# RNN, LSTM, shared MLP, experts and a low-rank adapter on one core: the first x tile by two transfers, the x tiles turned one to a step, and the fill work of an LSTM step dealt out anew

## The reference, cut to what matters

```python
x = x + rnn(x, h0=cond)        # h = tanh(h @ Wh + x_t @ Wx + b), 256 steps
x = x + lstm(x, h0=cond, c0=0) # gates i, f, o, g of 256 each, 256 steps
x = x + moe(x, cond)           # shared MLP 256 -> 1024 -> 256 on every token,
                               # and 2 of 4 experts of the same size, chosen per batch
x = x + adapter(x, cond)       # low rank 8, matrices made from LayerNorm(cond)
```

## Time and profile before

| what | value |
| --- | --- |
| median of 3 runs | 1104.92 us (1102.71 to 1107.42) |
| the profiled execution | 1103.3 us, of it 1101.5 us from first to last instruction |
| granted TensorE clock, mean | 0.987 of full speed |
| TensorE busy | 1064.8 us (97%) |
| VectorE, ScalarE, GpSimd busy | 75%, 59%, 26% |

### The profile page before, as it was taken

The page is one execution under the profiler, slowest core; times in us unless marked ns, Lnnn a source line. Parts: engine busy times, 40 slices in busy tenths (PEclk is TensorE's granted clock), DMA queues, the critical chain, the costliest instruction groups (busy, mean ns, idle before and its releaser), DMA issues. The chain is left out here.

```text
span 1101.5 us, 56333 instructions
## 1 busy us (share of the span) xinstructions
PE 1064.8 (97%) x22306; PEld 968.1 (88%) x22306; DVE 826.0 (75%) x3573; ACT 646.7 (59%) x2500; POOL 284.4 (26%) x862
## 2 busy tenths in 40 slices
PE   4899999999999999999999998899999999999998
PEld 3889899899999999999999997788888888888887
DVE  6577778878878878877887887876666666676797
ACT  4467767767777777777776765433333333343486
POOL 3223333333333333333333330560000000000041
PEclk9789999999999999999999999999999999999999
DMA  8401211211211200000000011100000000000022
GB/s 269 101 24 55 66 28 53 66 29 52 66 45 35 66 27 10 18 24 14 14 19 4 5 30 14 13 9 2 2 2 2 1 2 2 2 4 1 4 91 83
DMA packets 55434, 37.28 MB, mean 34 GB/s; under 512 B 25816, under 2 KB 54026, under 8 KB 55180
## 3 DMA queue, kind: packets, MB, share of 16 engines
q1 hardware_dynamic: 54316, 33.26, 10.8%
q10 hardware_dynamic: 864, 0.43, 0.2%
HBM read 28.68 MB, written 4.98 MB: 31 GB/s over the span
## 5 line engine op out<-in xcount | busy, mean ns | idle before, releaser
L670 ACT ACTIVATE gel<-bank,seq 128x256 f32<-128x256 f32 x256 | 121.2, 474 | 214.9 <-PE bank L1306 212.1
L1304 PE MATMUL bank<-XHL,WE 128*128 128x256 f16 x768 | 209.4, 273 | 2.6 <-DVE XHL L896 1.1
L1304 PE MATMUL bank<-GH,WE 128*128 128x256 f16 x768 | 209.3, 273 | 2.5 <-DVE GH L923 2.0
L1306 PE MATMUL bank<-XHL,WE 128*128 128x256 f16 x768 | 209.5, 273 | 0.0
L1305 PE MATMUL bank<-GH,WE 128*128 128x256 f16 x768 | 209.4, 273 | 0.0
L1306 PE MATMUL bank<-GH,WE 128*128 128x256 f16 x768 | 209.4, 273 | 0.0
L1305 PE MATMUL bank<-XHL,WE 128*128 128x256 f16 x768 | 209.4, 273 | 0.0
L464 POOL TENSOR_TENSOR RH<-rf,RH 128x32 f16<-128x32 f32 x256 | 73.3, 286 | 420.5 <-ACT RH L608 420.5
L1304 PE MATMUL bank<-seq 128*128 128x64 f16 (+2 forms) x1216 | 154.0, 202 | 1.8 <-DVE oz L956 1.1
L1306 PE MATMUL bank<-seq 128*128 128x64 f16 (+2 forms) x1216 | 154.5, 202 | 0.3 <-issue 0.3
L930 DVE CAST GH<-gel 128x256 f16<-128x256 f32 x256 | 78.1, 305 | 101.8 <-ACT gel L670 101.0
(11 more groups left out here) (221 smaller groups left out, 3353.9 us busy)
## 6 DMA issues: line engine op xcount, KB each, us to landing
stage<-in_L_cond_ew SPq DMA_DIRECT2D x64, 128.0 KB, 2.4
stage<-in_L_cond_W SPq DMA_DIRECT2D x32, 256.0 KB, 3.7
WE<-in_x SPq DMA_DIRECT2D x8, 512.0 KB, 10.0
out<-WE SPq DMA_DIRECT2D x16, 256.0 KB, 2.1
stage<-in_L_cond_sw SPq DMA_DIRECT2D x2, 1024.0 KB, 7.0
scratch<-rows SPq DMA_DIRECT2D x96, 8.0 KB, 1.9
stage<-in_L_cond_Wx SPq DMA_DIRECT2D x1, 1024.0 KB, 7.0
stage<-in_L_cond_Wh SPq DMA_DIRECT2D x1, 1024.0 KB, 9.4
```

Source lines behind the costliest of these rows:

```text
L670: nc.scalar.activation(gel[:, m % 2, :], banks[m % len(banks)][:, 0:256], ACT.Gelu_apprx_tanh, scale=scale, bias=bias).then_inc(s["a_g"], 1)
L1304: MM(out_, w(HI), x(HI), start=start, stop=False, skip_group_check=True)
L1306: return MM(out_, w(HI), x(LO), start=False, stop=stop, skip_group_check=True)
```

## The change

Seven edits:
1. `load_first` issues one transfer of 128 KB on each of the two queues in place of eight of 16 KB.
2. GpSimd's low halves of every second turn (k odd) move from RNN step 4k + 4 to 4k + 5.
3. In VectorE's start, the low halves of the first x tile and the copy of `lnT` move ahead of the RNN's bias rows.
4. Tiles 0 to 3 are turned beside RNN steps 3, 4, 6 and 7, tiles 4 to 7 after LSTM steps 1 to 4 of block 0, tiles 8 to 15 after steps 7 to 14 as before. Tiles 0 and 1 are copied out beside the RNN's start, 2 and 3 in step 0, 4 to 7 in steps 2 to 5.
5. `x_hi` and `x_lo` of block 0 move from steps 4, 6 and 5, 7 to steps 5, 6 and 6, 7.
6. `HALVES` and `HALVES_LOW` move half tiles out of steps 7 and 15, into 8 and 9 or into 9 and 13; `X_TILES` moves one gate tile from step 5 to step 7 of every eight.
7. `EXPERT` moves two weight pieces a block from steps 11 and 13 to 9 and 12 (blocks 9 and later); `block_sum` moves from steps 0 and 3 to 3 and 12.

```diff
-        def load_first(engine, batches):
-            for b in batches:
-                engine.dma_start(xin_first[U * (b % G):U * (b % G) + U, b // G, :], a["x"][b, 0:U, :]
+        def load_first(engine, halves):
+            for h in halves:
+                engine.dma_start(xin_first[:, h, :], a["x"][h * G:(h + 1) * G, 0:U, :]
                                  ).then_inc(s["ld_xf"], 16)
...
-                load_first(sp, range(G))
+                load_first(sp, (0,))
...
-                if n >= H and n % H == 0:
+                if n % G == H or (n > G and n % G == 1):
                     split_x1(n // H - 1, LO)
...
-                load_first(act, range(G, B))
+                load_first(act, (1,))
...
@@ ScalarE, the eight RNN steps at the start
+                if n == 5:
+                    x_out(0)
...
@@ ScalarE and VectorE, block_steps
-                    if it < NB - 1 and u in X_HI:
-                        x_hi(it + 1, X_HI.index(u))
+                    x_at = X_HI_FIRST if first else X_HI
+                    if it < NB - 1 and u in x_at:
+                        x_hi(it + 1, x_at.index(u))
...
@@ VectorE, the start
-            bias_parts(4 * D, 5 * D, S_RNN)
-            dve.sem_inc(s["v_const"], 1)
+            dve.wait_ge(s["v_xr"], 1)
+            V.tensor_tensor(XR[:, LO, 1], X[:, 1, :, 0:U].rearrange("p b t -> p t b"),
+                            XR[:, HI, 1], ALU.subtract).then_inc(s["v_xr"], 1)
             dve.wait_ge(s["pe_cond"], 2)
             V.tensor_copy(lnT[:].rearrange("p c b -> p (c b)"), cond_bank[:, C * B:2 * C * B]
                           ).then_inc(s["v_cond"], 1)
-            dve.wait_ge(s["v_xr"], 1)
-            V.tensor_tensor(XR[:, LO, 1], X[:, 1, :, 0:U].rearrange("p b t -> p t b"),
-                            XR[:, HI, 1], ALU.subtract).then_inc(s["v_xr"], 1)
+            bias_parts(4 * D, 5 * D, S_RNN)
+            dve.sem_inc(s["v_const"], 1)
             weight_lo(0, rnn_piece())
...
             for piece in range(N_LSTM):
                 weight_lo(N_RNN + piece, lstm_piece(piece))
+                if piece == 9:
+                    x_out(1)
...
@@ TensorE
-            pe.wait_ge(s["ld_xf"], 16 * B)
+            pe.wait_ge(s["ld_xf"], 16 * 2)
...
             for n in range(LAG):
                 rnn_step(n)
+                for k in X_TURN_FIRST[n]:
+                    transpose_x(k)
...
-            for k in X_OUT[0]:
-                transpose_x(k)
...
-                    if first and u + 1 < U:
-                        for k in X_OUT[u + 1]:
-                            transpose_x(k)
+                    for k in X_TURN[u] if first else ():
+                        transpose_x(k)
...
-HALVES = [0, 3, 2, 1, 3, 2, 2, 3, 0, 3, 2, 1, 3, 2, 2, 3]
-HALVES_LOW = [0, 3, 2, 1, 3, 2, 2, 3, 1, 3, 3, 1, 2, 1, 2, 3]
+HALVES = [0, 3, 2, 1, 3, 2, 2, 2, 1, 4, 2, 1, 3, 2, 2, 2]
+HALVES_LOW = [0, 3, 2, 1, 3, 2, 2, 2, 1, 4, 3, 1, 2, 2, 2, 2]
...
+X_HI_FIRST, X_LO_FIRST = (5, 6), (6, 7)
+X_TURN_FIRST = [(), (), (), (0,), (1,), (), (2,), (3,)]
+X_TURN = [(), (4,), (5,), (6,), (7,), (), (), (8,), (9,), (10,), (11,), (12,), (13,), (14,), (15,), ()]
-X_OUT = [(2 * u, 2 * u + 1) if u < 4 else (u,) if u >= 8 else () for u in range(U)]
+X_OUT = [(2, 3), (), (4,), (5,), (6,), (7,), (), ()] + [(k,) for k in range(8, 16)]
...
-           [], [("ig", 0), ("o", 0), ("o", 1)], [("f", 0), ("f", 1), ("ig", 1)], [("ig", 2), ("ig", 3)]]
-EXPERT, EXPERT_LOW = (1, 11, 13, 15), (1, 9, 12, 14, 15)
-SUMS, SUMS_LAST, ADD_Y = (0, 3), (0, 1), (1, 2)
+           [], [("o", 0), ("o", 1)], [("f", 0), ("f", 1), ("ig", 0)], [("ig", 1), ("ig", 2), ("ig", 3)]]
+EXPERT, EXPERT_LOW = (1, 9, 12, 15), (1, 9, 12, 14, 15)
+SUMS, SUMS_LAST, ADD_Y = (3, 12), (0, 1), (1, 2)
```

More of the change, by code:

```diff
@@ L1070, in block_steps @@
                         extras[u]()
-                    if it < NB - 1 and u in X_LO:
-                        x_lo(it + 1, X_LO.index(u))
+                    x_at = X_LO_FIRST if first else X_LO
+                    if it < NB - 1 and u in x_at:
+                        x_lo(it + 1, x_at.index(u))
                     for k in X_OUT[u] if first else ():
```

## The result

The changed kernel takes 1097.61 us (median of 5 runs, 1096.15 to 1098.6) against 1104.92 before, a ratio of 0.993 with a 95% interval of 0.9909 to 0.9952. Timed once more beside the experiments it took 1097.97 against 1104.37: 0.9952 (0.9935 to 0.997). So it is 6 to 7 us faster by the medians, and the time is inside the predicted range. (The ratios are estimated from all executions and are not the quotients of these medians; their intervals reach from 3 to 10 us.) The working behind the 1095 holds less well than the number. One execution of the kernel `a_sw` further down took 1866.07 us and is not counted in its ratio; why it was so slow isn't known.

The account below looks back on a forecast made before the run. Each LSTM step was taken as ended by TensorE's own list or the step's chain (floor 2.31 us). From 1103.3 us, -3.5 - 4.3 + 0.2 - 0.8 + 0.2 = -8.2 gave 1095.1 us, range 1091.5 to 1099.5.

Parts of the forecast that it names:

- start: Up to the first LSTM step: 3.1 us from earlier transfers plus 0.4 from VectorE's order, 29.31 to 25.8 us.
- these have the same company on the queues as before, so they come about 3.1 us earlier: At the start: the adapter's first weights still land 5.2 us after issue, so about 3.1 us earlier; bounds 1.5 and 3.3.
- the start gives less: Rival at the start: gain only 1.5 us, start and weights' landing slip by 1.6, total 1096.7 us; chance 0.12.
- VectorE's new order: At the start: the `lnT` copy starts at 12.7, not 13.17, bringing the first RNN product 0.4 us earlier; bounds 0 and 0.5.
- Turning the tiles: Tiles turned beside RNN steps: block 0's steps 0 to 3 need 10.3 us, with no TensorE wait for an x copy.
- the prediction's first rival: Half clock in block 0's steps 2 and 3: step 4 starts about 3 us later, total 1096.7 us; chance 0.14.
- The wait for the MLP's weights: Block 0, before step 4's gates: ScalarE waits from about 36 us for weights landing near 37.9; step 5 starts at 39.8.
- the term of step 13: Blocks 9 to 14: two VectorE operations of 0.42 us just ahead of `ig` lengthen step 13 by about 0.10 us.
- GpSimd's move: Low halves moved beside TensorE-bound steps 2 and 10 cost nothing there; bound +0.15 us in each, 4 us over 14 blocks.
- holds up `ig`: Step 1 of blocks 1 to 14: `block_sum` delays `ig`; moving it and GpSimd's low halves out of step 0 gives -0.20 us.
- The rival by which the gate tiles come too late: GpSimd's low halves come too late in step 2 or 10: 31 turns lose 0.4 us each, total 1107; chance 0.05.
- The end: Last block: a half tile moved into step 9 and a wait at the end that doesn't shrink, +0.2 us.

Follow-up runs that it names:

- a_sw: Changed kernel with SP's fourteen small tables moved from ahead of the shared MLP's weight loads to behind them; ratio 0.9902 to the kernel before.
- after: The changed kernel with all seven edits, first measurement and first trace; 1097.61 us against 1104.92 before, ratio 0.993.
- a_again: The changed kernel timed and traced again with no edit; 1097.97 us against 1104.37 before, ratio 0.9952.
- b_blocks: Kernel before with only the moved half tiles, gate tiles, GpSimd low halves, expert pieces and block sums; ratio 0.999.
- b_pool: Kernel before with only GpSimd's low halves of every second turn one RNN step later, one line; ratio 0.9967.
- b_sums: Kernel before with only VectorE's two block sums moved from steps 0 and 3 to 3 and 12; ratio 0.9975.
- b_halves: Kernel before with only the new tables of half tiles, gate tiles and expert pieces; ratio 1.0008.
- b_start: Kernel before with only the two large first x transfers and VectorE's new order at the start; ratio 0.9998.
- b_turn: Kernel before with only the new turning, copying and splitting of block 0's x tiles; ratio 0.9981.
- a_all: Changed kernel with adapter weights ahead of ScalarE's small tables, MLP weights ahead of SP's, and tiles 4 to 7 copied a step earlier; 1095.52 us, ratio 0.9914.
- a_aw1: Changed kernel with the adapter's first weights ahead of the small tables on ScalarE's queue; ratio 0.9938 to the kernel before.

## Why the number was right and what in it was wrong

The table gives each term. For what the change leaves, I take the mean of `after` and `a_again`; for the kernel before, the mean of the traces that have that part unchanged.

| term | predicted | measured | from |
| --- | --- | --- | --- |
| start | -3.5 | -1.2 | 28.78 against 29.97 (before, b_blocks, b_pool, b_sums, b_halves) |
| block 0, steps 0-3 | -5.6 | -5.7 | 10.65 against 16.33 (before, b_start, b_sums, b_halves) |
| block 0, steps 4-15 | +1.5 | +2.5 | 36.59 against 34.08 (before, b_start, b_sums) |
| blocks 1-14 | -0.8 | -3.6 | 559.44 against 563.04 (before, b_start, b_turn) |
| block 15 and after | +0.2 | +1.0 | 460.15 against 459.13 (before, b_start, b_turn) |

The measured terms add up to -7.0 us; the medians say -7.3 and -6.4. That the total fits is partly luck: the start gave 2.3 us less than forecast and blocks 1 to 14 gave 2.8 us more, from unrelated steps of the working. The measured -1.2 of the start is uncertain too, since among the five traces with the old start the first LSTM step lies between 28.89 and 30.93 us.

- **The start failed.** The step "these have the same company on the queues as before, so they come about 3.1 us earlier" was wrong. The issues moved by 2.4 and 2.9 us, since one large transfer took 1.22 and 0.80 us to issue and not 0.47. The landing moved by 0.36: 7.3 us after the issue in place of 5.2. The adapter's weights are now issued 0.74 us ahead of SP's first 1 MB transfer (3.51 and 4.25), where it was 1.2. `b_start` shows that the start alone gives nothing that its timing can tell. The term stood outside its own bound of 1.5, and the rival "the start gives less" is what happened. That the nearer 1 MB transfer delays them is argued from these rows; no run moves it alone. The working also missed that VectorE waits for these weights only by the shared count `ld_first`. VectorE's new order was right, and worth a little more than its bound of 0.5: from L879 to the `lnT` copy it takes 1.40 us instead of 1.96.
- **Turning the tiles was right**, in size too: steps 0 to 3 of block 0 at 2.30, 2.46, 2.51 and 2.92 us against 2.3, 2.7, 2.4 and 2.9, and no wait for a copy. `b_turn` shows it by itself. But these are the steps of the first trace, the only one of seven kernels built on the change that has the full clock there (`b_turn` has it too). In the other six step 2 runs partly at half clock and takes 3.4 to 3.7 us. That is the prediction's first rival in a milder form: steps 0 to 3 are 0.9 us longer in `a_again`, not 3, and the wait for the weights is shorter.
- **The wait for the MLP's weights came, and its length by luck** (1.73 us, forecast near 1.9). The forecast had ScalarE there from about 36 us and the data at 37.9; it came at 38.8 and the data at 40.45, 2.8 and 2.6 us late. SP's issue moved by 1.6 us and the landing by 0.5, since the transfer took 6.2 us in place of 5.1. What the wait costs is 0.0 to 0.4 us by the traces of `a_sw` and `a_again`. Missed was the second wait: `x_hi` needs tile 7, whose copy stands in VectorE's step 5. I had costed the crowding of these steps at 0.4 us without asking which tile `x_hi` waits for.
- **Blocks 1 to 14 were mis-sized** by 2.8 us. Step by step the sum for blocks 9 to 14 was -0.04 and came out at -0.30. Nearly all of the difference is the term of step 13: predicted +0.10, measured -0.14. I costed `block_sum` in step 12 as two more operations ahead of `ig`; `b_sums` shows that they cost nothing (2.49), and the runs of single pieces show that step 13 gains only when a gate tile and an expert piece have left it and a block sum stands in step 12. Blocks 1 to 8 came out at -0.12 against -0.07, as good as predicted. Over 14 blocks that makes 8 x -0.12 + 6 x -0.30 = -2.8; the other 0.8 is in single stalls, among them block 1 (41.17 to 40.53).
- **GpSimd's move** was costed at nothing. With step 1 freed by it, `b_pool` alone is 3.0 us faster by the median; I had given that gain to `block_sum` and GpSimd together, and either would have done; that `block_sum` "holds up `ig`" was not a cause, since `ig` is as late in `b_pool`. The step's 0.20 us over 14 blocks is the whole 2.8 us of the typical blocks: the losses and gains of the moved fill work cancel. The rival by which the gate tiles come too late did not happen: step 2 is 2.58 as before.
- **The end** cost 0.8 us more than predicted. Step 9 of block 15 takes 4.01 us here and 3.36 before, and the rest 420.9 or 422.2; neither is a fixed price of an edit: step 9 takes 2.80 in `b_blocks` and `b_halves`, which have the new tables, at a clock of 1.00 against 0.69 here, and `a_again` has 420.9. The rest follows the clock: in the four traces with 422.1 to 422.2 the granted clock is 0.83 in the 10 us behind the last LSTM step, and in the other ten, all at 420.8 to 421.0, it is 1.00. First the changed kernel's first trace, then `a_again`:

```profile
674.56:684.56 10.00, 8.25 (x92) 5.72 (x92) 6.57 (x30) 5.11 (x11) 0.00 (x0) 0.83 0.13 12
673.46:683.46 10.00, 7.24 (x94) 5.42 (x95) 6.77 (x31) 6.36 (x14) 0.00 (x0) 1.00 0.12 12
```

All four are kernels built on the changed one (4 of 7); whether these meet the half clock there more often is open.

## What to carry to other kernels

A transfer that is issued 2.4 us earlier may land only 0.1 to 0.4 us earlier; don't carry its time to landing over from the old order when bulky transfers move up with it. Ask which of several small transfers will be last, and whether the operation that waits reads them all: one semaphore for four transfers makes every reader wait for the last. Time each part of a change alone: in this case the one line that moves GpSimd's low halves and the turning of the tiles account for most of it. Where two engines slow one another, look at which starts first in each of the steps: moving either piece of work by a step can be enough, and then the second move buys nothing there. In a stretch that runs partly at half clock, take a second trace of the same kernel before an edit is blamed for 2 us or a shorter wait is credited with 1.

## What the runs showed of the hardware that I had not expected

- A transfer of 1 KB landed 3.5 to 6.7 us after its issue with the first 1 MB transfer issued 0.7 to 1.7 us behind it (3.5 before, 4.5 in the changed kernel and in `a_all`, 6.7 in `a_aw1`). `a_all` and `a_aw1` issue the same transfers at the same times up to there.
- A transfer of 256 KB landed 5.2 us after its issue before, with the first 1 MB transfer 1.2 us behind it, and 7.3 and 7.6 us in the two traces of the changed kernel, with it 0.74 us behind.
- One transfer of 128 KB took ScalarE's queue 1.22 us and SP's 0.80 us to issue; eight of 16 KB took 3.70 and 3.65.
- With the same instructions, steps 8 to 15 of block 0 took 25.21 us at a granted clock of 0.67 to 0.76 and 23.15 at 0.85, and what follows the recurrence took 422.2 or 420.9 with 0.83 or 1.00 in its first 10 us.
- A VectorE operation of 0.18 us took 0.34 to 0.36 when it started 0.03 to 0.05 us behind GpSimd's low halves, and 0.19 when it started 0.01 or 0.09 us ahead of them. GpSimd's starts are rough in a trace.
